# Last layer of a four-layer graph network: eight gather buffers, and own rows made behind each table

## What is computed

```python
h = jnp.maximum(_layernorm(x, axis=-1), 0.0)
# L3: src, tgt = the two ends of every edge; W is 512 x 1024
x_ij = jnp.concatenate([h[src], h[tgt]], axis=1)
m_ij = jax.nn.relu(x_ij @ W.T + b)
x = x + jax.ops.segment_sum(m_ij, src, num_segments=625)
```

## Time and profile before

| | us |
|---|---|
| median of 3 runs | 1257.53 (1257.19 to 1258.17) |
| the profiled execution | 1254.69 |
| its span, first to last instruction | 1252.9 |
| PE busy | 1147.2 (92%) |
| DVE busy | 832.3 (66%) |
| ACT busy | 556.0 (44%) |
| POOL busy | 519.1 (41%) |

### The profile page before, as it was taken

One profiled execution on the slowest core, in us unless ns is written; L12 is line 12 of the kernel. 1 busy time (PEld: TensorE's weight loads), 2 busy tenths in 40 slices (PEclk: granted clock), 3 DMA queues, 4 the chain that ended last, 5 costly groups with the idle time before them and its releaser, 6 DMA issues. The chain is left out here.

```text
span 1252.9 us, 15171 instructions
## 1 busy us (share of the span) xinstructions
PE 1147.2 (92%) x4406; PEld 600.4 (48%) x4411; DVE 832.3 (66%) x1902; ACT 556.0 (44%) x971; POOL 519.1 (41%) x444
## 2 busy tenths in 40 slices
PE   3678888999999998999999999999999999958887
PEld 1143223345444445555555555555555474434554
DVE  5985885691233234777787877877777678437777
ACT  1212223102002112677777777777777541124444
POOL 1000112333433303778666666666663000366650
PEclk9879999999999998999999999999999999969999
DMA  7998996473110033955444444444441010355551
GB/s 276 381 376 341 367 354 235 167 257 112 46 43 14 26 127 108 238 138 110 94 93 97 92 98 93 93 95 92 98 92 22 19 53 9 105 172 162 162 166 41
DMA packets 61141, 177.42 MB, mean 142 GB/s; under 512 B 12773, under 2 KB 13317, under 8 KB 53256
## 3 DMA queue, kind: packets, MB, share of 16 engines
q0 software_dynamic: 32496, 76.65, 25.4%
q1 hardware_dynamic: 28568, 99.80, 21.5%
HBM read 161.36 MB, written 15.05 MB: 141 GB/s over the span
## 5 line engine op out<-in xcount | busy, mean ns | idle before, releaser
L1322 PE MATMUL PS<-wide,hidT 128*128 128x512 f32 x696 | 312.8, 592 | 0.0
L601 POOL DMA_INDIRECT rec_scratch<-rec_src,slot_row x84 | 99.2, 1181 | 245.4 <-DMA rec_scratch<-rec_src,slot_row 207.4
L1322 PEld LDWEIGHTS PS<-wide,hidT 128*128 128x128 f32 x696 | 131.6, 189 | 132.5 <-issue 125.2
L1143 POOL DMA_INDIRECT pair_sum<-table_j,counts_rec x87 | 146.7, 1686 | 27.6 <-issue 26.2
L1255 ACT ACTIVATE wide<-PS 128x512 f32<-128x512 f32 x174 | 103.9, 597 | 118.6 <-PE PS L1305 81.0
L1135 POOL DMA_INDIRECT pair_sum<-table_i,counts_rec x87 | 87.7, 1008 | 137.9 <-PE PS L1305 77.9
L1438 POOL DMA_INDIRECT u_space<-table_j,wide x87 | 87.7, 1008 | 130.5 <-DMA table_j<-agg_rows 83.5
L1260 ACT ACTIVATE wide<-wide,two 128x512 f32<-128x512 f32 x174 | 124.9, 718 | 6.1 <-issue 3.5
L1193 DVE SCALAR_TENSOR_TENSOR wide<-wide 128x512 f32<-128x512 f32 x174 | 120.5, 692 | 6.0
L1265 ACT ACTIVATE wide<-wide 128x512 f32<-128x512 f32 x174 | 109.7, 630 | 5.5
L1152 POOL DMA_INDIRECT rec_scratch<-rec_src,slot_row x84 | 89.8, 1070 | 37.2 <-issue 23.2
(11 more groups left out here) (246 smaller groups left out, 1833.2 us busy)
## 6 DMA issues: line engine op xcount, KB each, us to landing
ring<-basis_rows SPq DMA_DIRECT2D x56, 1024.0 KB
ring<-basis_low SPq DMA_DIRECT2D x30, 256.0 KB, 6.5
w_scratch<-stage SPq DMA_DIRECT2D x112, 32.0 KB
rec_scratch<-ring POOLq DMA_DIRECT2D x2, 1496.0 KB, 13.8
counts_rec<-rec_scratch SPq DMA_DIRECT2D x1, 2992.0 KB, 9.4
rec_scratch<-rec_src,slot_row POOLq DMA_INDIRECT x168, 2.2
root<-L_gnn_root SPq DMA_DIRECT2D x2, 1024.0 KB
rows_in<-in_rows_in SPq DMA_DIRECT2D x2, 1024.0 KB, 18.6
```

The lines of the kernel that those rows point to most:

```text
L601: nc.gpsimd.indirect_dma_start(out=rec3_dram, out_offset=bass.IndirectOffsetOnAxis(ap=slot_row[:, 1, t:t + 1], axis=0), in_=rec, in_offset ...
L1143: nc.gpsimd.indirect_dma_start(out=pair_sum[:, t % GOT3, :], out_offset=None, in_=tables[0][1], in_offset=bass.IndirectOffsetOnAxis(ap=idx ...
L1322: m = nc.tensor.matmul(o, hidT[:, t % 2, k * P:(k + 1) * P], w2[:, k, :], start=False, stop=(k == KT - 1), skip_group_check=True)
```

## The change

`GOT5`, the number of gather buffers in the last layer, goes from 20 to 8. And `table_rows`, `low_part`, `high_part`, `table_of` and `self_of` of chunk 2 move into the loops over the chunks on DVE, ACT and PE, so that the own part of chunk 2 is made behind its table, and ahead of the turn of chunk 4 and the tables of chunks 3 and 4. Behind the loops remain both tables and both own parts of chunks 3 and 4.

```diff
-            GOT5, HOT5, PAIR5, SPLIT5, TURN_GROUP = 20, 16, 6, 3, 4
+            GOT5, HOT5, PAIR5, SPLIT5, TURN_GROUP = 8, 16, 6, 3, 4
@@ DVE
                     rows_of(1, c, x_rows)
-                    if 2 <= c < NT - 1:
+                    if c >= 2:
                         table_rows(c - 2)
                         low_part(c - 2)
-                for c in range(NT - 3, NT):
-                    table_rows(c)
-                for c in range(NT - 3, NT):
-                    low_part(c)
+                table_rows(NT - 2)
+                table_rows(NT - 1)
+                low_part(NT - 2)
+                low_part(NT - 1)
@@ ACT
-                    if 2 <= c < NT - 1:
+                    if c >= 2:
                         high_part(c - 2)
                     turned4(c)
-                for c in range(NT - 3, NT):
-                    high_part(c)
+                high_part(NT - 2)
+                high_part(NT - 1)
                 turned(0)
@@ PE
-                for c in range(NT - 3):
+                for c in range(NT - 2):
                     table_of(c)
                     self_of(c)
                     turn4(c + 2)
-                table_of(NT - 3)
                 table_of(NT - 2)
-                turn4(NT - 1)
                 table_of(NT - 1)
-                for c in range(NT - 3, NT):
-                    self_of(c)
+                self_of(NT - 2)
+                self_of(NT - 1)
```

## The result

| | before | after |
|---|---|---|
| median, us | 1257.53 (5 runs, 1256.30 to 1260.67) | 1247.08 (5 runs, 1242.95 to 1252.66) |
| ratio | | 0.9913, 95% interval 0.9892 to 0.9934 |
| the profiled execution | 1254.69 | 1243.66 |
| its span | 1252.9 | 1241.9 |

In this measurement the kernel became 0.9% faster, and 1245.5 us was forecast. That is not the whole result: on the five chips that the experiments ran on, neither the change (repeated on one of them) nor its parts and other numbers of buffers do anything that can be told from the noise. The record doesn't say which chip the result itself was measured on. First the profile after, as it answers to the rows of before.

A forecast was written before the change was run, and what follows sets the result against it. Taken as the bound: a hidden backlog in the last layer's tile loop, served at a fixed rate. Between gains of 10.3 and 15.1 us, 12.0 was taken: 1257.5 - 12.0 = 1245.5 us, range 1239 to 1262, own range to 1251.

The forecast's parts named there:

- Part 1: Making of tables in the last layer: chunk 2's own rows go earlier, so the first gather comes 2.7 us later.
- Part 2: Own rows on PE: a 0.69 us gap goes, add 0 comes at 1093.0 instead of 1093.68; bounds -0.7 to +0.0.
- Part 3: Last layer's tile loop: eight buffers instead of twenty shrink the starting backlog; with the moved own rows, 12.0 us gained.
- The two ends of the sum: Tile loop: gain 10.3 us if the backlog is served from first gather, 15.1 if the middle pace runs from add 0.
- the service reading: Tile loop: each gather costs 1.38 us, other tile work 0.22, so 137.4 us from first gather to add 79.
- A: Start of the tile loop: the first four tiles take 24.3 us again whatever the buffers; slower, 1262 us; chance 0.19.
- C: Tile loop: waits vanish once POOL is tied eight tiles behind; 1.306 us a tile, gain 38 us, 1219.5; chance 0.07.
- D: Gather ring of eight too short: late gathers make the pace 1.7 us, gain some 4 us, 1254; chance 0.07.
- Something is served at a fixed rate: Middle of the tile loop: regular waits put down to issue, read as a hidden backlog pacing tiles at 1.598 us.
- rival B: Tile loop: waits absent from timed runs, 1.306 us a tile throughout; only add 0 counts, -0.7 us, 1256.8; chance 0.13.
- the backlog reading: Tile loop: gathers fill a hidden backlog faster than it drains, delaying other engines' waits; 1.38 us per gather, 0.22 other work.

## Why the prediction was right, and why that is not enough

**Part 1, the moved own part: right.** From the first table's start (1051.55 before, 1053.62 after) to the first gather it is 32.4 and 35.0 us, 2.6 later, where 2.7 were worked out; `turned4(4)` and `low_part(2)` cost nothing.

**Part 2, add 0: right.** From the same mark to add 0, 42.1 and 41.3 us: 0.9 sooner for 0.7. On the quiet chip it is 42.0 and 41.1 (first tables at 1057.95 and 1060.91). This is all that the change gives there, and it is less than the runs can tell.

**Part 3, the buffers: right in that measurement.** The two ends of the sum were gains of 10.3 and 15.1 us in the stage, and 12.0 was taken. From the first table to the last add it fell from 191.9 to 178.8 us, 13.1; the late start of 2.1 us leaves 11.0 in the span. The first four tiles gave 14.1 us, and the 82 steps behind add 4 took 1.9 more (125.5 before, 127.4 after), since twelve tiles more ran beside gathers. Of the two readings between which 12.0 was picked, neither came out exactly. By the service reading add 79 follows the first gather by 137.4 us, and it was 135.0 (1088.60 to 1223.56); by the other it follows add 0 by 126.2, and it was 128.7. That the time is so close is owed to the choice between them, which was a judgement. The agreement of the service reading with before (134.8 us) was no test of it, as its two terms had been fitted to that trace.

A and C did not happen there: add 4 came early, and the waits on issue were not fewer. D is less plain, because with landings missing no wait could be given a gather's name. Against it stands that the longest wait of an add in after (5.3 us, ahead of add 4) is for PE, which had itself stood for 3.2 us with nothing named, and `own` does not wait for a gather.

**What failed is the step from the rows to the program.** "Something is served at a fixed rate" was read as the kernel's own bound. The rate was real in that trace, and the sum built on it came out. But on five chips the same kernel takes 1221.5 to 1228.6 us, and the traces taken there, of before on one of them and of its variants on all, have no such rate, with twice the traffic neither. So the price of rival B, -0.7 us, is the one that holds on those chips (0.9 in the traces), though its pace of 1.306 us is not: beside gathers it is 1.34. In the measurement of the result B did not hold. That the forecast came out is luck in this sense: it was tied to the one measurement with the waits, and would have missed on each of the five chips. B was held down by one sentence, that the timed runs take as long as the profiled one. That sentence proves less than it was given: every timed run of the result comes with a span and a granted clock of its own, from which I infer that records were written in each. Timed and profiled run would then share whatever clogs.

Two readings of the rows were off as well. The 32.1 us on issue in 40 cases are not all lost time: on the quiet chip the same kernel has 13.7 us in 37. And that all engines stand still holds for the end of the longest wait and not for the waits in general: in the one ahead of the add at 1198.37, PE works until 1198.38 by its modelled ends, and the DMA engines are busy for 0.42 of 1197.5 to 1198.0 and 0.73 of 1198.0 to 1198.4.

**What can be said of the cause.** Shown: with the waits the loop takes 34.6 us more in before and 22.2 in after (137.5 less 115.3); landings are missing in both of these traces, in before already in the layer ahead; neither 3.7 times the updates nor 386 GB/s makes the waits on a quiet chip. Argued only: that writing the records is what holds the engines there. The rule of the Trainium skill quoted ahead (NOTIFIC — the notification-queue block, "Overflow: three behaviours, one of which stalls the engine") would allow such waits, and fewer gathers in flight would then help by spreading records. The traces neither show the holding back nor exclude it: landings are missing both where engines were held and where they were not. Two rivals stay open beside it: something else on that chip or at that moment, and semaphore updates that reach the engines late. No run here was made without records, and none met the waits again. Why eight buffers cost less there stays with the backlog reading, which fits one pair of traces.

## What to carry to other kernels

Waits of 2 us and more that name nothing and come on several engines are a reason to measure on a second chip before a sum is built on them. A DMA without a landing time in the profile is a weaker hint, since landings went missing here without any wait too. The depth of a gather ring follows from the trip of a gather and the pace: with four buffers a gather has three tiles, 3 x 1.34 = 4.0 us, for the wake of POOL (0.3) and its trip from the start of the issue (3.7 in the median, 4.9 at most), which was just too little. Six were enough, and eight carried a trip of 6.3 us. A PE that is busy for 112.2 of 115 us, as in the loop of after on the quiet chip, gains nothing from a better feed.

## What the runs showed of the hardware that was not expected

The same program took 1257.5 us in one measurement and 1221.5 to 1228.6 on the five chips of the experiments, and one loop accounts for all of the difference and more (34.6 us). Landing records can be lost by the hundred in a stretch that runs at full speed. A gather of 256 KB lands in 3.7 us after the start of its issue at 195 GB/s, in 6.3 at 386 GB/s, and in 2.8 at half the width. Full DMA engines cost the tile loop 1 us of 115, in one run.
